# Swapping two copies on ScalarE: turned probabilities first, finished output chunk second

## What is computed

```python
def _causal_attn(q, k, v, scale):
    s = jnp.einsum('bhqd,bhkd->bhqk', q, k) * scale
    s = jnp.where(mask[None, None], s, jnp.finfo(s.dtype).min)
    p = jax.nn.softmax(s, axis=-1)
    return jnp.einsum('bhqk,bhkd->bhqd', p, v)
...
attn = _causal_attn(q, k, v, SCALE)
lat = _causal_attn(q, lk, lv, SCALE)
return attn @ w_o + lat @ w_lo
```

## Time and profile before

| | |
|---|---|
| median of 3 runs | 2124.37 us (2123.72 to 2124.85) |
| profiled execution, its own time | 2122.39 us |
| its span in the trace | 2120.6 us |
| TensorE busy | 2026.5 us (96%) |
| VectorE busy | 1409.2 us (66%) |
| ScalarE busy | 1044.6 us (49%) |
| GpSimd busy | 1060.2 us (50%) |

### The profile page before, as it was taken

One profiled execution on the slowest core, in us unless ns is written; L12 is line 12 of the kernel. 1 busy time (PEld: TensorE's weight loads), 2 busy tenths in 40 slices (PEclk: granted clock), 3 DMA queues, 4 the chain that ended last, 5 costly groups with the idle time before them and its releaser, 6 DMA issues.

```text
span 2120.6 us, 39951 instructions
## 1 busy us (share of the span) xinstructions
PE 2026.5 (96%) x12832; PEld 1824.3 (86%) x12832; DVE 1409.2 (66%) x3404; ACT 1044.6 (49%) x2461; POOL 1060.2 (50%) x873
## 2 busy tenths in 40 slices
PE   6999999999999999999999999999999999999995
PEld 5988889888898888988898898988989888898883
DVE  5757757576675757757577675767757576575766
ACT  3644626355363644626356373554626456273651
POOL 4536465364644537445364554536455364653630
PEclk9999999999999999999999999999999999999998
DMA  5010010100001000010100001010010100100001
GB/s 169 1 33 11 2 54 1 43 1 31 24 1 43 2 32 24 1 43 1 54 1 21 23 1 54 1 33 11 2 54 1 33 11 21 34 1 31 1 11 40
DMA packets 19367, 50.86 MB, mean 24 GB/s; under 512 B 5824, under 2 KB 7872, under 8 KB 19008
## 3 DMA queue, kind: packets, MB, share of 16 engines
q1 hardware_dynamic: 19136, 48.00, 6.8%
HBM read 45.89 MB, written 2.10 MB: 23 GB/s over the span
## 4 chain that ended last, share of the span: by engine, by line
PE 45%; issue 27%; POOL 24%; DVE 3%; POOLq 0%; ACT 0%; DVEq 0%; ACTq 0%
POOL probs L672 14%; PE ps L315 13%; PE ps L316 13%; PE ps L317 13%; PE ps L402 6%; POOL probs L663 4%; POOL ql_lo L667 4%; POOL pt_lo L648 1%; DVE pt_lo L679 1%; DVE stats L804 0%; POOLq L671 0%; PE ps L495 0%; PE ps L510 0%; POOL wlk_lo L654 0%; DVE probs L715 0%
## 5 line engine op out<-in xcount | busy, mean ns | idle before, releaser
L672 POOL TENSOR_TENSOR probs<-probs,inv_sum 128x640 f32<-128x640 f32 (+7 forms) x512 | 586.3, 1147 | 493.8 <-DVE inv_sum L746 493.1
L679 DVE TENSOR_TENSOR pt_lo<-ps,pt_hi 128x512 fp32r<-128x512 f32 (+3 forms) x768 | 401.6, 551 | 202.8 <-ACT pt_hi L517 199.6
L549 ACT ACTIVATE probs<-probs,neg_max 128x640 f32<-128x640 f32 (+7 forms) x512 | 397.6, 777 | 163.5 <-DVE neg_max L739 163.5
L517 ACT ACTIVATE pt_hi<-ps 128x512 fp32r<-128x512 f32 (+3 forms) x768 | 347.1, 486 | 185.3 <-PE ps L402 171.9
L739 DVE CUSTOM_DVE_ANT_0 probs<-ps,mask 128x640 f32<-128x640 f32 (+7 forms) x512 | 384.1, 753 | 57.6 <-PE ps L317 37.2
L315 PE MATMUL ps<-pt_hi,val_hi 128*128 128x256 f32 (+1 forms) x1280 | 371.0, 290 | 31.2 <-DVE pt_lo L679 31.2
L316 PE MATMUL ps<-pt_lo,val_hi 128*128 128x256 f32 (+1 forms) x1280 | 359.7, 281 | 0.0
L317 PE MATMUL ps<-pt_hi,val_lo 128*128 128x256 f32 (+1 forms) x1280 | 358.8, 280 | 0.0
L402 PE MATMUL ps<-ident,probs 128*128 128x128 f32 x2304 | 337.2, 274 | 15.4 <-POOL probs L672 13.3
L402 PEld LDWEIGHTS ps<-ident,probs 128*128 128x128 f32 x2304 | 266.1, 140 | 49.8 <-POOL probs L672 18.7
L315 PEld LDWEIGHTS ps<-pt_hi,val_hi 128*128 128x128 f32 x1280 | 242.5, 189 | 56.5 <-issue 55.0
(11 more groups left out here) (107 smaller groups left out, 4214.7 us busy)
## 6 DMA issues: line engine op xcount, KB each, us to landing
raw<-wo SPq DMA_DIRECT2D x32, 512.0 KB, 3.3
raw<-wq SPq DMA_DIRECT2D x16, 512.0 KB, 3.3
raw<-wlv SPq DMA_DIRECT2D x16, 512.0 KB, 3.9
raw<-wkv SPq DMA_DIRECT2D x8, 512.0 KB, 3.5
acc<-xT SPq DMA_DIRECT2D x4, 512.0 KB, 5.9
acc<-x SPq DMA_DIRECT2D x1, 2048.0 KB, 7.6
wlk_raw<-wlk SPq DMA_DIRECT2D x16, 128.0 KB, 4.0
out<-acc SPq DMA_DIRECT2D x8, 256.0 KB, 2.4
```

The costliest lines, as they stand in the source:

```text
L517: return nc.scalar.activation(dst, src, ACT.Copy)
L549: nc.scalar.activation(dst, dst, ACT.Exp, bias=neg_max[:, n % 8:n % 8 + 1], scale=-1.0, accum_out=row_sum[:, n % 8:n % 8 + 1]).then_inc(q[ ...
L672: nc.gpsimd.tensor_tensor(b, b, inv_sum[:, k % 8:k % 8 + 1].to_broadcast([P, b.shape[-1]]), ALU.mult).then_inc(q["normed"], 1)
L679: return nc.vector.tensor_tensor(dst, src, h, ALU.subtract)
```

## The change

Within a slot, ScalarE makes the high parts of the turned probabilities first and that of the finished chunk, with its output weights where it has any, second. The other engines' programs are the same.

```diff
                     for k in range(SLOTS):
+                        if 0 <= k - T_LAG < TILES:
+                            probs_hi(g, pair, k - T_LAG)
                         if k in O_SLOT:
                             output_hi(g, pair, O_SLOT[k])
-                        if 0 <= k - T_LAG < TILES:
-                            probs_hi(g, pair, k - T_LAG)
                         if EARLY <= k < TILES:
                             exponentials(g, pair, k)
```

## The result

| | before | changed |
|---|---|---|
| median | 2124.11 us (6 runs) | 2132.82 us (6 runs) |
| range of the runs | 2123.72 to 2124.85 | 2131.32 to 2134.12 |
| ratio, 95% interval | | 1.0041 (1.0028 to 1.0054) |
| profiled execution, own time | 2122.39 us | 2133.48 us |
| its span | 2120.6 us | 2131.4 us |

The change costs 8.7 us by the medians. The forecast was 2132.8 us. Its agreement with the median to the last digit is luck: the six runs spread over 2.8 us.

A forecast was written before the change was run, and what follows sets the result against it. The prediction took TensorE, busy 96% of the span, to bound the kernel. Slot 34 alone costs 0.53 us a pass, 16 x 0.53 = 8.5 us, on the median 2124.37: 2132.8 us (+0.4%), range 2130.0 to 2138.2.

The forecast's parts named there:

- What bounds the kernel, and that only 14 slots change: TensorE bounds, 96% busy; ScalarE's order matters only through TensorE's waits; only even slots 8 to 34 change, 14 a pass.
- Slots 8 to 32 at nothing: In slots 8 to 28, 30 and 32 of each pass, the new order delays nothing that reaches TensorE: 0 us.
- the delay, forecast at 0.07 us: Slot 12: VectorE's low part of the chunk starts some 0.07 us late, taken up in VectorE's 0.28 us idle time.
- The cover of 0.11 us: Slot 12: ScalarE is free at 854.35, 0.11 us before the row maximum lets the exponential go.
- The forecast sign that these exponentials still wait for the maximum by about 0.1 us: Slots 12, 20 and 28: the profile after still shows exponentials waiting for `neg_max`, by only about 0.1 us.
- For slot 30 the text had the probabilities' copy start as soon as ScalarE is free: Slot 30: that copy starts 0.78 us earlier, three copies together take as long, the exponential does not move: 0.
- Slot 34, link by link: Slot 34: probabilities' copy waits for the turned block, weights' low part 1.01 us late, TensorE's product late: 0.53 us a pass.
- the new wait: Slot 34: TensorE's product waits for the last block's low part, 905.47 instead of 904.99: 0.48 us a pass.
- The profiled execution: Whole kernel: the one profiled execution goes from 2122.39 to 2130.9 us.
- B: Copies do not overlap when swapped; exponentials of slots 12, 20, 28 also 0.11 us late: 5.3 us more, 2138.1; chance 0.12.
- D: Earlier copies of odd tiles shrink three TensorE waits a pass: net gain 4.0 us, 2120.4; chance 0.03.
- C: Slot 34: the 0.66 us slack before TensorE's product holds, nothing measurable (+0 to +4 us); chance 0.07.

The follow-up runs named there:

- experiment 1: Kernel before with the new copy order in 13 of the 14 slots, the old order kept in slot 34: 2123.59 us, ratio 0.9999.
- experiment 6: Changed kernel plus an extra 256-column ScalarE copy ahead of the exponential in slots 12, 20 and 28: 2140.07 us, ratio 1.0079.
- Experiment 2: Kernel before with the new copy order in slot 34 alone: 2133.08 us, ratio 1.0042.
- 3: Kernel before, but in slot 34 only the weights' copy goes behind the probabilities' copy (chunk, probabilities, weights): 2129.06 us, ratio 1.0023.
- experiment 4: Changed kernel, but in slot 34 VectorE makes the last tile's low part before the weights' low part: 2123.85 us, ratio 0.9999.
- experiment 5: Kernel before plus an extra 256-column ScalarE copy ahead of the exponential in slots 12, 20 and 28: 2123.93 us, ratio 1.0001.
- experiments 5 to 8: Experiment 5, experiment 6, and the kernel before with the next long tile copied ahead of the exponential in three slots (2101.47 us) or seven (2082.98 us).

## Why the prediction was right

- **What bounds the kernel, and that only 14 slots change**: right. ScalarE's added idle time of 70 us for turned blocks (171.9 to 242.4) moved nothing except in slot 34.
- **Slots 8 to 32 at nothing**: shown by experiment 1, ratio 0.9999. Slot 12 of the changed kernel, ScalarE and VectorE, for the earlier trace rows:

```profile
857.85 0.60 ACT L517 ACTIVATE pt_hi<-ps 128x512 fp32r<-128x512 f32 x1 [0.42 <-PE ps L402]
858.35 0.38 ACT L517 ACTIVATE o_hi<-ps 128x256 fp32r<-128x256 f32 x1
858.73 1.05 ACT L549 ACTIVATE probs<-probs,neg_max 128x896 f32<-128x896 f32 x1
```

```profile
858.76 0.42 DVE L679 TENSOR_TENSOR o_lo<-ps,o_hi 128x256 fp32r<-128x256 f32 x1
...
860.38 1.02 DVE L679 TENSOR_TENSOR pt_lo<-ps,pt_hi 128x512 fp32r<-128x512 f32 x2 [0.19 <-ACT pt_hi L517]
```

The exponential starts 0.88 us after the probabilities' copy, as before, and VectorE's idle time ahead of 860.38 is 0.19 instead of 0.28: the delay, forecast at 0.07 us, is 0.09 and is absorbed where it was expected to be. The cover of 0.11 us came out at 0.12 in experiment 6. The forecast sign that these exponentials still wait for the maximum by about 0.1 us did not show as such: the chunk's copy ends at 858.73 and the exponential starts then, so the rows have no idle time there. The cover lies in the overlap that this pair does not use, and only experiment 6 measures it. The ScalarE overlap that keeps it is in these rows: 857.85 + 0.60 against 858.35, 0.10 us, where the Trainium skill (ScalarE: Activation LUTs, What ACT_TABLE_LOAD costs) has 93 ns. Its Read-Write Bubble (Advanced Engine Details and Errata, TRN2 Errata), read as no overlap at all, doesn't hold for these copies.
One thing was overlooked here. For slot 30 the text had the probabilities' copy start as soon as ScalarE is free. That holds in pair 0; in pair 1 the turned block is later, ScalarE waits for it, so the three copies end later, and the idle time before the exponential, 0.29 us before, is down to 0.03:

```profile
1021.63 0.49 ACT L517 ACTIVATE pt_hi<-ps 128x384 fp32r<-128x384 f32 x1 [0.15 <-PE ps L402]
...
1022.94 1.15 ACT L549 ACTIVATE probs<-probs,neg_max 128x1024 f32<-128x1024 f32 x1
```

The maximum still decides when the exponential starts, so it cost nothing. (And where the text of slot 34 speaks of the first and last of the 16 stretches, its rows are those of the seventh and the last; the first has the same slack in the trace.)
- **Slot 34, link by link**: right. The last block's low part was forecast 1.01 us late and is 1.03; the new wait was forecast at 0.48 and is 0.49 to 0.50, with 0.05 behind it. 16 x 0.54 = 8.6 us (8.8 by the starts of the passes), against 8.5 forecast and 8.7 measured. Experiment 2 has it alone, 3 has half of it with the weights' low part 0.75 us late (906.67 against a turn at 905.10) instead of 1.02, so that the slack takes up 0.54 of either delay, and 4 takes it away by the one queue position that it hangs on.
- **The profiled execution** was forecast at 2130.9 and took 2133.48. The passes explain 8.8 of the 11.1 us. Nearly all of the rest is at both ends of the kernel, outside the change (last section), and the median of six runs doesn't show it.
- **Rivals**: B and D were excluded by 1. B's mechanism exists: once 0.3 us more work stands in those slots, the exponential is late and TensorE with it by the same amount, 0.18 us a place (experiment 6; B had 0.11). B's cause, copies that do not overlap in the new order, isn't there: they do. D needed ScalarE to release the exponential, and experiment 1 gained nothing. C fell with the 16 new waits.

## What to carry to other kernels

A reorder on an engine that is half idle isn't free of risk: find, for each place, the instruction that is queued behind the moved one on the next engine, and compare the delay with its slack; 13 of 14 places had the slack and the 14th cost all of it, through an unrelated 1.2 us instruction between two that mattered. Cover that a change uses up without cost is gone for the next change: 0.26 us of it went here, and an addition that was free before then cost 7 us. To gain time, start from the bounding engine's waits and go back to what stands between the ready data and its consumer. Here that was an exponential ahead of copies that TensorE needed first, worth 1.9%.

## What I had not expected

The first 40 us differ between executions of kernels that have the same program there. Busy times by engine, then granted clock, DMA share and GB/s, for that stretch: before; the changed kernel; experiment 4; experiment 5.

```profile
0.00:40.00 40.00, 23.82 (x99) 19.71 (x100) 18.87 (x25) 12.72 (x16) 16.12 (x19) 0.91 0.70 223
```

```profile
0.00:40.00 40.00, 24.42 (x93) 19.83 (x94) 17.84 (x24) 12.13 (x16) 15.07 (x19) 0.87 0.70 223
```

```profile
0.00:40.00 40.00, 23.25 (x97) 19.20 (x98) 18.44 (x25) 12.72 (x16) 15.71 (x19) 0.91 0.68 223
```

```profile
0.00:40.00 40.00, 24.68 (x93) 20.04 (x94) 17.82 (x24) 12.12 (x16) 15.05 (x19) 0.87 0.70 223
```

The granted clock is 0.91 or 0.87 of full speed, a mix of the two levels, with no relation to the order of copies: experiment 5 has the order of before and 0.87, experiment 4 the changed order and 0.91. The changed kernel's profile has the lower one. It reaches the second pass 1.57 us later than the kernel before, of which 0.55 is slot 34 and 1.0 is the start; behind the first matmul of the last pass it needs 1.5 us more, again 0.55 for slot 34 and 1.0 at the end, where 40 us in the layer norms have 0.80 against 0.82. I put these 2 us down to the clock at both ends, but did not test it, and the start isn't explained by it alone: experiment 2, with 0.91, is 0.8 us late there beyond its own slot 34. Over many runs the whole time goes with the clock of the run: of the 15 runs of the kernel before that were timed beside experiments 5 to 8, the two with a mean clock of 0.995 took 2120.79 and 2121.29 us, the seven with 0.992 2123.78 to 2125.64. A difference of that size in one profiled execution should not be charged to a change before the stretches without it have been compared.
